# Two stacked graph layers on one core: V as three one-pass products, raw loaded behind P, graph 0 with rows first

## The chip, the cores and the metric

One Trainium2 chip, one core. The metric is the device time of one execution in microseconds (us), the median of several runs. A profile is one execution of its own.

## The reference, cut to what matters

Eight graphs (b) of C = 1024 nodes with D = 256 features, and an adjacency of 1024x1024 that is mostly zeros. All is float32.

```
L0:  H = (adj != 0); w = adj[0, :]                      # first row as edge weights
     Dn = 1 / (H @ w);  Be = 1 / H.sum(axis=0)
     conv(x, W, b) = Dn * (H @ (Be * (H.T @ (x @ W.T)))) + b
     h = layer_norm(relu(conv(x, W1, b1)), gamma, beta) # W1: 512x256
     y = conv(h, W2, b2) + x                            # W2: 256x512
x1 = layernorm(x + y)
L1:  agg = (adj @ x1) / max(adj.sum(-1), 1e-6)
     out = relu(concat(x1, agg) @ WL.T)                 # WL: 256x512
result = layernorm(x1 + out)
```

## The kernel before

Everything is tiled by 128 nodes: NT = 8 tiles a graph. The five engines each run an instruction order written out by hand, and wait for each other on semaphores; one engine's order is a queue that nothing overtakes. The stages of a graph, in TensorE's order, are these.

- **S1**: H transposed times x (x in two parts, x_hi and x_lo, each good for one pass of TensorE in the type float32r), one PSUM bank a tile. A column of ones beside x_hi gives the degrees for rBe. ScalarE copies a tile out as m_hi (`take_m_hi`), the vector engine as m_lo (`take_m_lo`).
- **S2**: HT (the transposed H) times m, in four jobs of 512 columns; split into z_high, z_low and z_cross.
- **M, P, TH, Q**, per tile: M is z_cross times W1_cross (two products), P is z_high times W1_high and z_low times W1_low (four products); `mm` writes 128x512 each. Together these six one-pass products give the exact float32 product. Then bias, relu, layer norm in the buffer hrow, its transposes (TH), and Q, the product with W2 in plain float32. The last three Q stand inside S3 (`last_of_Q`).
- **S3**: H times q (`take_q` on the vector engine, x_hi on ScalarE, x_lo on GpSimd), again out as m_hi and m_lo.
- **S4**: HT times m; the vector engine adds the residual (xres), makes bn_stats and bn_aggr, ScalarE the root (`root`), the vector engine its inverse and the centring (`centre`): this is x1, in xres. S4 computes tiles 0 and 1 together and then one tile after another. Ahead of the last tile's products TensorE transposes x1(0) and x1(1) (`before_last`).
- **V**: x1 transposed (TX, two transposes a tile) and copied to x1T by ScalarE, times WLT, in plain float32: two products a tile, each of which is two instructions in the trace. x1T has two slots. ScalarE copies the bank into yv.
- **L**: adjT times the right half of yv, in plain float32, and the final norm. The vector engine transposes the next graph's adjB blocks between.

Banks: PRODUCT_BANKS names the bank of each product. The transposes TH and TX take banks 6 and 7 in turn. A job waits until the bank's last user has been emptied (`free`, `emptied`, `full`). `over_graphs` loops over graphs; `more` is true for all but the last.

Beside this run the preparations for the next graph. SP issues the loads: w_row, x_in, then after the last Q raw (the 4 MB adjacency in the space that z and hrow leave, four pairs of tiles, four transfers each), then adjB tile by tile behind `H_ready` and `dn_ready`. The vector engine makes the degree sums (`sum_Dn`, a product of raw != 0 with w_row and a row sum): five among the last m_lo of S3, three during V. It also builds the eight H tiles (`build_H_tile`) during V. ScalarE splits the next x (`split_x_hi`) after S3, GpSimd subtracts (`split_x`) and later makes the residual.

Graph 0 has a setup of its own: it loads plain rows tile by tile, transposes them on TensorE (two sets of four 128x128 blocks a tile) between S1's products of tiles 0 to 5 (N_SIDE = 6 banks), and at places given by BETWEEN transposes the weights as well. Banks 6 and 7 are used in turn there too.

Of the kernel before, what the change touches and what calls it, by code (L numbers as in the profile page):

```python
# [11 lines left out]
P = 128  # L12
# [22 lines left out]
N_BANKS = 8  # L35
# [4 lines left out]
DN_LAG = 3  # L40


def graph_net(nc, x, adj, W1, b1, gamma, beta, W2, b2, WL, out):
# [21 lines left out]
    BETWEEN = {1: ("gamma",), 3: ("W1", "W1"), 5: ("WL", "WL"), NT - 1: ("W2", "W2")}  # L65
# [50 lines left out]
    for i in range(NT + 1):  # L116
        if i < NT:
            add_job("TX", i)
        if i > 0:
            add_job("V", i - 1)  # L120
    for i in range(NT):
        add_job("L", i)

    ctx = ExitStack()
    with ctx:
# [13 lines left out]
        H, _, _ = place("H", [P, NT, C], F32R)  # L139
# [3 lines left out]
        x_lo, _, _ = place("x_lo", [P, NT, D], F32R)  # L143
        m_hi, m_hi_at, _ = place("m_hi", [P, NT, D], F32R)
        m_lo, _, _ = place("m_lo", [P, NT, D], F32R)
        x_in, _, _ = place("x_in", [P, NT, D], F32)
        xres, xres_at, _ = place("xres", [P, NT, D], F32)
# [10 lines left out]
        x1T, _, _ = place("x1T", [P, 2, ND, P], F32, q_at)  # L158
        ident, _, _ = place("ident", [P, P], F32)
        small, _, _ = place("small", [P, 21, NT], F32)  # L160
# [13 lines left out]
        unread_V, _, _ = place("unread_V", [P, C], F32, nxt)  # L174
        unread, _, _ = place("unread", [P, C], BF16, q_at)

# [6 lines left out]
        W1T, _, _ = place("W1T", [P, ND, DH], F32, xres_at)  # L183

        def col(n):
# [3 lines left out]
         std_o, rstd_o, gb, rDn_main, rDn_cross, shift_h) = (col(n) for n in (*range(16), 18, 19, 20))  # L189
        gamma_c, bW2_c, eps_c = gb[:, 0:NH], gb[:, NH:NH + ND], small[:, 16, 0:1]  # L190
        stats, _, _ = place("stats", [P, NT, 6], F32)
# [3 lines left out]
        banks = [ctx.enter_context(nc.psum_tensor(f"bank{n}", [P, 512], F32)) for n in range(N_BANKS)]  # L195

        def sem(name):
# [10 lines left out]
        x_loaded, w_loaded, W2_loaded, W1_loaded, WL_loaded, gamma_loaded, beta_loaded, bias_loaded, table_loaded = (  # L208
            sem(n) for n in ("x_loaded", "w_loaded", "W2_loaded", "W1_loaded", "WL_loaded",
                              "gamma_loaded", "beta_loaded", "bias_loaded",  # L210
                              "table_loaded"))
        ident_zero, ident_ready, eps_ready, ones_ready, x_split, x_hi_done, xb_part, xb_ready = (
            sem(n) for n in ("ident_zero", "ident_ready", "eps_ready", "ones_ready", "x_split", "x_hi_done",
# [8 lines left out]
        W1_high_done, W1_low_done, W1_low_scaled, W1_cross_done = (  # L222
            sem(n) for n in ("W1_high_done", "W1_low_done", "W1_low_scaled", "W1_cross_done"))
# [61 lines left out]
        def _(sp):  # L285
            def load_graph(b):
                for j in range(NT // 2):
                    for a in range(NB):
# [35 lines left out]
            load_first_rows(4)  # L324
            load_first_x(3)
            load_first_rows(5)
            sp.dma_start(WLn[:, :, :], WL.rearrange("(t p) d -> p t d", p=P)).then_inc(WL_loaded, 16)
            load_first_rows(6)
            load_first_rows(7)
            sp.dma_start(W2n[:, :, :], W2.rearrange("(t p) d -> p t d", p=P)).then_inc(W2_loaded, 16)  # L330
            sp.dma_start(beta_row[:, :], beta.partition_broadcast(P)).then_inc(beta_loaded, 16)
            sp.dma_start(b1_row[:, :], b1.partition_broadcast(P)).then_inc(bias_loaded, 16)
            sp.dma_start(b2_row[:, :], b2.partition_broadcast(P)).then_inc(bias_loaded, 16)

            def graph(b, more, first):
                if more:
# [5 lines left out]
                    sp.wait_ge(*full("Q", NT - 1, b))  # L342
# [28 lines left out]
        def _(pool):  # L371
            nc.gpsimd.memset(ident[:, :], 0.0).then_inc(ident_zero, 1)
            nc.gpsimd.memset(x_hi[:, :, D:DP].bitcast(F32), 1.0).then_inc(ones_ready, 1)
            nc.gpsimd.memset(eps_c, NORM_EPS).then_inc(eps_ready, 1)
# [19 lines left out]
            for j in range(NT // 2):  # L394
                pool.wait_ge(first_x_loaded[j], 16)
# [33 lines left out]
        def _(act):  # L429
# [87 lines left out]
            def graph(b, more):  # L517
# [46 lines left out]
                if more:  # L564
                    split_x_hi(b + 1)
# [534 lines left out]
```

## Time and profile before

| | before |
|---|---|
| median of 3 runs | 1089.66 us (1089.65 to 1089.69) |
| profiled execution | 1090.12 us |
| its span, first to last instruction | 1088.5 us |
| mean granted TensorE clock | 0.999 of full speed |
| TensorE busy | 1073.5 us (99%) |
| vector engine, ScalarE, GpSimd busy | 746.4, 372.7, 217.5 us (69%, 34%, 20%) |
| chain that ended last, by engine | TensorE 91%, vector engine 6%, DMA 1% |

The profiled execution is about 1.6 us longer than its span (start and end of the program). In the profile PE is TensorE's products, PEld its weight loads, DVE the vector engine, ACT ScalarE, POOL GpSimd, SP the engine that issues most loads. A row's duration runs from the start of an instruction to its end; following instructions of the same engine overlap by some tenths of a microsecond, so the distance from one start to the next is what an instruction costs its queue. The same line can serve several stages, so rows are told apart by their tiles and shapes.

### The profile page before, as it was taken

Reading aid. Unit: us, or ns where it says so; the run is one execution under the profiler, and the core shown is the slowest. Engines: PE = TensorE matmul, PEld = TensorE weight load, DVE = VectorE, ACT = ScalarE, POOL = GpSimd, SP = SyncE. Lnnn points to the kernel's source line nnn. Section 1 sums busy time; section 2 is a strip of 40 time slices with the busy share of each in tenths; the row PEclk is TensorE's granted clock in tenths of the full one; section 3 lists DMA queues with packets and bytes.
Section 4 is the critical chain, followed back from the end, with each engine's and each line's share of the span. In section 5 each row is a group of like instructions: output and inputs, shape, how many; then the busy total and the mean of one; then the engine's idle time right before and its main releaser. Section 6 shows DMA issues by size and latency. Waiting matters only on the chain.

```text
span 1088.5 us, 18849 instructions
## 1 busy us (share of the span) xinstructions
PE 1073.5 (99%) x6235; PEld 919.3 (84%) x6235; DVE 746.4 (69%) x1972; ACT 372.7 (34%) x811; POOL 217.5 (20%) x276
## 2 busy tenths in 40 slices
PE   7899999999999999999999999999999999999997
PEld 7789698896988969898798978989789896888966
DVE  6875596665965768758687486774867747867326
ACT  5372213622145321453115431154302533026230
POOL 1623004220041202312032120411204120041000
PEclk9999999999999999999999999999999999999999
DMA  8207712076210662125611355115542065300001
GB/s 295 59 1 156 155 42 57 0 154 155 57 40 24 130 157 55 39 54 121 143 48 39 83 126 117 41 39 112 128 87 68 9 142 127 68 11 1 1 1 39
DMA packets 63871, 86.44 MB, mean 79 GB/s; under 512 B 8164, under 2 KB 53864, under 8 KB 63848
## 3 DMA queue, kind: packets, MB, share of 16 engines
q1 hardware_dynamic: 63376, 85.75, 34.4%
q10 hardware_dynamic: 472, 0.40, 0.1%
q8 instruction: 13, 0.21, 0.1%
q14 instruction: 10, 0.08, 0.0%
HBM read 77.73 MB, written 8.39 MB: 79 GB/s over the span
## 4 chain that ended last, share of the span: by engine, by line
PE 91%; DVE 6%; DMA 1%; issue 1%; ACT 0%; SPq 0%; DVEq 0%
PE bank L882 41%; PE bank L993 10%; PE bank L1056 10%; PE bank L975 10%; PE bank L912 8%; PE bank L1023 3%; PE bank L1028 3%; PE bank L1029 3%; PE bank L1001 3%; PE bank L1041 1%; DMA raw<-in_adj_dram 1%; DVE adjT L666 1%; DVE unread L618 1%; DVE HT L671 1%; DVE m_lo L653 1%
## 5 line engine op out<-in xcount | busy, mean ns | idle before, releaser
L882 PE MATMUL bank<-yv,adjT 128*128 128x257 f32 x1024 | 223.3, 379 | 0.0
L882 PEld LDWEIGHTS bank<-yv,adjT 128*128 128x128 f32 x1024 | 193.6, 189 | 31.8 <-issue 3.8
L469 ACT ACTIVATE small<-mv,small 128x1 f32<-128x1 f32 x192 | 56.6, 295 | 348.8 <-DVE mv L648 248.8
L403 POOL TENSOR_TENSOR xres<-x_in 128x256 f32<-128x256 f32 x64 | 45.6, 748 | 410.3 <-DMA out_dram<-xres 406.8
L882 PE MATMUL bank<-x_hi,H 128*128 128x256 f32 x512 | 126.0, 287 | 0.0
L912 PE MATMUL bank<-x_hi,H 128*128 128x258 f32 x512 | 123.8, 289 | 1.9 <-DVE x_lo L702 1.4
L882 PE MATMUL bank<-x_lo,H 128*128 128x256 f32 x512 | 122.4, 280 | 0.0
L993 PE MATMUL bank<-gW2T,xnT 128*128 128x256 f32 x512 | 122.1, 381 | 0.0
L882 PE MATMUL bank<-m_hi,HT 128*128 128x256 f32 x512 | 121.6, 280 | 0.0
L882 PE MATMUL bank<-m_lo,HT 128*128 128x256 f32 x512 | 120.9, 279 | 0.0
L912 PE MATMUL bank<-x_lo,H 128*128 128x256 f32 x512 | 119.3, 282 | 0.1
L1056 PE MATMUL bank<-WLT,x1T 128*128 128x512 f32 x256 | 119.1, 593 | 0.0
L464 ACT ACTIVATE m_hi<-bank,small 128x256 fp32r<-128x256 f32 x128 | 58.3, 477 | 164.1 <-DVE small L698 96.9
L993 PEld LDWEIGHTS bank<-gW2T,xnT 128*128 128x128 f32 x512 | 95.1, 189 | 13.4
L653 DVE SCALAR_TENSOR_TENSOR m_lo<-bank,small,m_hi 128x256 fp32r<-128x256 f32 x128 | 59.4, 480 | 68.4 <-ACT m_hi L464 68.4
L975 PE MATMUL bank<-HT,m_hi 128*128 128x512 f32 x256 | 101.2, 395 | 1.1 <-DVE m_lo L653 1.0
L975 PE MATMUL bank<-HT,m_lo 128*128 128x512 f32 x256 | 101.6, 397 | 0.0
L882 PEld LDWEIGHTS bank<-x_hi,H 128*128 128x128 f32 x512 | 96.8, 189 | 0.2
L882 PEld LDWEIGHTS bank<-x_lo,H 128*128 128x128 f32 x512 | 96.3, 188 | 0.2
L882 PEld LDWEIGHTS bank<-m_lo,HT 128*128 128x128 f32 x512 | 96.1, 188 | 0.0
L882 PEld LDWEIGHTS bank<-m_hi,HT 128*128 128x128 f32 x512 | 96.1, 188 | 0.0
L912 PEld LDWEIGHTS bank<-x_hi,H 128*128 128x128 f32 x512 | 93.4, 190 | 3.1 <-DVE H L603 2.3
(102 smaller groups left out, 1814.4 us busy)
## 6 DMA issues: line engine op xcount, KB each, us to landing
raw<-in_adj_dram SPq DMA_DIRECT2D x112, 256.0 KB, 8.6
adjB<-in_adj_dram SPq DMA_DIRECT2D x224, 128.0 KB, 3.4
x_in<-in_x_dram SPq DMA_DIRECT2D x31, 256.0 KB, 4.6
out_dram<-xres SPq DMA_DIRECT2D x108, 64.0 KB, 1.6
raw<-in_adj_dram SPq DMA_DIRECT2D x8, 512.0 KB, 10.4
w_row<-in_adj_dram SPq DMA_DIRECT2D x8, 512.0 KB, 3.7
out_dram<-xres SPq DMA_DIRECT2D x4, 256.0 KB, 2.2
W1n<-in_L_gnn_W_dram SPq DMA_DIRECT2D x1, 512.0 KB, 11.0
```

Source lines behind the costliest of these rows:

```text
L403: nc.gpsimd.tensor_tensor(xres[:, t, :], x_in[:, t, :], x_in[:, t, :], ALU.add).then_inc(xb_part, 1)
L464: nc.scalar.activation(m_hi[:, e, :], bank(stage, e)[:, 0:D], ACT.Identity, scale=rBe[:, e:e + 1])\
L469: nc.scalar.activation(std[:, i:i + 1], mv[:, which, i, 1:2], ACT.Sqrt, bias=eps_c)\
L653: empties_bank(nc.vector.scalar_tensor_tensor(out=m_lo[:, e, :], in0=bank(stage, e)[:, 0:D], scalar=rBe[:, e:e + 1], in1=m_hi[:, e, :].bit ...
L882: last = mm(bank(stage, i)[:, 0:n_cols], lhsT, rhs, start=(k == 0 and part == 0), stop=(k == NT - 1 and part == parts - 1))
L912: last = mm(*args, start=(c == 0 and n == 0), stop=(c == NT - 1 and n == 1))
L975: last = mm(bank("S2", job)[:, :], m[:, k, d * P:(d + 1) * P], HT[:, k, ch * CH:(ch + 1) * CH], start=(k == 0 and n == 0), stop=(k == NT - ...
L993: last = mm(bank("Q", i)[:, 0:D], xnT[:, k, :], gW2T[:, k, :], start=(k == 0), stop=(k == NH - 1))
L1001: last = nc.tensor.transpose(bank("TH", i)[:, k * P:(k + 1) * P], hrow[:, i % H_SLOTS, k * P:(k + 1) * P], ident[:, :])
L1023: last = mm(bank("M", s)[:, :], z_cross[:, d, nodes], W1_cross[:, d, :], start=(d == 0), stop=(d == ND - 1))
L1028: mm(bank("P", s)[:, :], z_high[:, d, nodes], W1_high[:, d, :], start=(d == 0), stop=False)
L1056: last = mm(bank("V", i)[:, :], x1T[:, i % 2, d, :], WLT[:, d, :], start=(d == 0), stop=(d == ND - 1))
```

## The change

V is split like M and P. WL becomes WL_high, WL_low and WL_cross once a graph (ScalarE and GpSimd, in the space of x_hi and x_lo, after S3), and x1 becomes x1_high, x1_low and x1_cross tile by tile in three slots: `take_x1` on ScalarE, `take_x1_low` on the vector engine (this one empties the TX bank), `take_x1_cross` on GpSimd. V takes four products, a new job VM two; yv is V's copy (times 1 + 1/4096) by ScalarE, less VM by the vector engine. x1(0) and x1(1) are transposed ahead of S4's last tile as before, x1(2) behind it, and then x1(i + 3) behind VM(i).

The centring of x1 (and of the result, except in the last graph) moves to ScalarE (`centre_rows`), with a shift from two small operations on GpSimd (`shift_of`). Six of the next graph's H tiles are built in S4 (H_LATE), two after V. raw's first three pairs are loaded behind the last P, the fourth behind the last Q. The degree sums: 0 ahead of q(7), 1 to 3 behind it, 4 to 7 around the last m_lo of S3 (DN_BEFORE). The split of the next x moves behind V.

In graph 0 the rows are loaded first and the weights last, and the weights' transposes stand in tiles 5 (W1), 6 (W2) and 7 (WL). W1_low and W1_cross are made by the vector engine, the residual by ScalarE (doubling) and GpSimd (b2). Degree sums 0 and 1 stand in the loop, 2 to 7 behind it, and six rBe are made in one go.

```diff
-    "V": (4, 5, 0, 1, 4, 5, 0, 1),
+    "V": (4, 0, 2, 4, 0, 2, 4, 0),
+    "VM": (5, 1, 3, 5, 1, 3, 5, 1),
...
+FIRST_DN = 2
+X1_SLOTS = 3
+H_LATE = 6
+DN_BEFORE = {4: (4,), 5: (5,), 7: (6,)}
...
-    BETWEEN = {1: ("gamma",), 3: ("W1", "W1"), 5: ("WL", "WL"), NT - 1: ("W2", "W2")}
+    BETWEEN = {1: ("gamma",), NT - 3: ("W1", "W1"), NT - 2: ("W2", "W2"), NT - 1: ("WL", "WL")}
...
+                    if j == 0:
+                        sp.wait_ge(*full("P", NT - 1, b - 1))
+                    elif j == NT // 2 - 1:
+                        sp.wait_ge(*full("Q", NT - 1, b - 1))
...
             load_first_rows(0)
+            load_first_rows(1)
             load_first_x(1)
-            load_first_rows(1)
             load_first_rows(2)
+            load_first_rows(3)
+            load_first_x(2)
+            load_first_rows(4)
             load_w(0)
-            load_first_x(2)
-            load_first_rows(3)
+            load_first_rows(5)
+            load_first_x(3)
+            load_first_rows(6)
             sp.dma_start(W1n[:, :, :], W1.rearrange("(t p) d -> p t d", p=P)).then_inc(W1_loaded, 16)
...
             load_first_rows(7)
...
+                for d in range(ND):
+                    pool.wait_ge(WL_high_done, b * ND + d + 1)
+                    nc.gpsimd.tensor_tensor(WL_low[:, d, :], WLT[:, d, :], WL_high[:, d, :].bitcast(F32),
+                                            ALU.subtract).then_inc(WL_low_done, 1)
...
+                def take_x1_cross(i):
+                    pool.wait_ge(*emptied("TX", i, b))
+                    n = i % X1_SLOTS
+                    nc.gpsimd.tensor_tensor(x1_cross[:, n, :], x1_high[n].bitcast(F32),
+                                            x1_low[:, n, :].bitcast(F32), ALU.subtract).then_inc(x1_cross_done, 1)
+
+                for i in range(NT):
+                    shift_of("1", 1, rstd_1, shift_1, mean_1_scaled, shift_1_done, i, b)
+                    if i >= NT - 2:
+                        take_x1_cross(i - (NT - 2))
+                for i in range(2, NT):
+                    take_x1_cross(i)
...
+                def take_x1(i):
+                    n = i % X1_SLOTS
+                    act.wait_ge(*full("TX", i, b))
+                    nc.scalar.activation(x1_high[n], bank("TX", i)[:, 0:D], ACT.Copy, scale=ROUND_DOWN)\
+                      .then_inc(x1_high_done, 1)
+                    nc.scalar.activation(x1_cross[:, n, :], bank("TX", i)[:, 0:D], ACT.Copy, scale=SPLIT * ROUND_DOWN)\
+                      .then_inc(x1_scaled, 1)
+
+                for i in range(NT):
+                    root("1", 1, std_1, i, b)
+                    if i > 0:
+                        centre_rows("1", rstd_1, shift_1, shift_1_done, i - 1)
+                    if i >= NT - 3:
+                        take_x1(i - (NT - 3))
+                centre_rows("1", rstd_1, shift_1, shift_1_done, NT - 1)
+                for i in range(NT):
+                    if i + 3 < NT:
+                        take_x1(i + 3)
+                    act.wait_ge(*full("V", i, b))
+                    empties_bank(nc.scalar.activation(yv[:, i, 0:2 * D], bank("V", i)[:, :], ACT.Copy,
+                                                      scale=1.0 + 1.0 / SPLIT), "V", i)
...
+                if c == NT - 3:
+                    sum_Dn(0, 0, unread, (first_rows_loaded[0], 16))
+                if c == NT - 2:
+                    sum_Dn(1, 0, unread, (first_rows_loaded[1], 16))
+                    take_W1_low(0)
+            take_W1_low(1)
+            sum_bW2()
+            take_W1_cross(0)
+            take_W1_cross(1)
+            sum_Dn(2, 0, unread, (first_rows_loaded[2], 16))
+            take_first_rBe()
+            take_m_lo("S1", 0, 0, 0)
             build_HT_columns(NT - 2)
...
+                next_Dn((0,), unread_Q)
                 take_q(NT - 1)
+                next_Dn((1, 2, 3), unread_Q)
...
                 for e in range(NT):
+                    if e in DN_BEFORE:
+                        next_Dn(DN_BEFORE[e], unread)
                     take_m_lo("S3", e, b, NT + e)
...
+                next_Dn((NT - 1,), unread)
+
+                def take_x1_low(i):
+                    n = i % X1_SLOTS
+                    dve.wait_ge(x1_scaled, b * NT + i + 1)
+                    empties_bank(nc.vector.scalar_tensor_tensor(
+                        out=x1_low[:, n, :], in0=bank("TX", i)[:, 0:D], scalar=SPLIT,
+                        in1=x1_cross[:, n, :].bitcast(F32), op0=ALU.mult, op1=ALU.subtract), "TX", i)
...
                         nc.vector.bn_stats(stats[:, i, :], xres[:, i, :]).then_inc(stats_done, 1)
-                    if i > 0:
-                        if i < NT:
+                    if i < NT:
+                        if more and 0 < i <= H_LATE:
                             dve.wait_ge(stats_done, b * NT + i + 1)
-                        centre("1", 1, xres[:, i - 1, :], rstd_1, i - 1, b)
-                    if i < NT:
-                        if i == 0:
+                            build_H_tile(i - 1, b + 1)
+                        elif i == NT - 1:
+                            dve.wait_ge(stats_done, b * NT + i + 1)
+                            take_x1_low(0)
+                        else:
                             dve.drain()
                         nc.vector.bn_aggr(mv[:, 1, i, :], stats[:, i, :]).then_inc(var_done["1"], 1)
-
+                take_x1_low(1)
+                take_x1_low(2)
                 nc.vector.memset(yv[:, :, 2 * D:YP], 1.0).then_inc(y_ones, 1)
...
+                transpose_x1(2)
+                pe.wait_ge(WL_cross_done, b * ND + ND)
 
                 for i in range(NT):
+                    n = i % X1_SLOTS
                     pe.wait_ge(*free("V", i, b))
                     pe.wait_ge(*emptied("TX", i, b))
                     for d in range(ND):
-                        last = mm(bank("V", i)[:, :], x1T[:, i % 2, d, :], WLT[:, d, :],
+                        part = slice(d * P, (d + 1) * P)
+                        mm(bank("V", i)[:, :], x1_high[n][:, part], WL_high[:, d, :], start=(d == 0), stop=False)
+                        last = mm(bank("V", i)[:, :], x1_low[:, n, part], WL_low[:, d, :],
+                                  start=False, stop=(d == ND - 1))
+                    fills_bank(last, "V", i)
+                    pe.wait_ge(*free("VM", i, b))
+                    pe.wait_ge(x1_cross_done, b * NT + i + 1)
...
+                    if i + X1_SLOTS < NT:
+                        transpose_x1(i + X1_SLOTS)
```

## Rows read from the trace of the kernel before

**Rows 1.** The page, busy time and share of the span by engine.
```profile
PE 1073.5 (99%) x6235; PEld 919.3 (84%) x6235; DVE 746.4 (69%) x1972; ACT 372.7 (34%) x811; POOL 217.5 (20%) x276
```

**Rows 2.** Windows, TensorE, S4 and V of graph 3: length, busy, clock, DMA.
```profile
494.70:510.15 15.45, 15.45 (x135) 1.00 0.49 105
510.15:525.20 15.05, 15.05 (x46) 1.00 0.70 164
```

**Rows 3.** Timeline, TensorE, into V of graph 3 (start, duration, what).
```profile
507.89 0.60 PE L1041 MATMUL bank<-ident,xres 128*128 128x128 f32 x4
510.15 1.88 PE L1056 MATMUL bank<-WLT,x1T 128*128 128x512 f32 x4
511.86 0.38 PE L1041 MATMUL bank<-ident,xres 128*128 128x128 f32 x2
```

**Rows 4.** Timeline, TensorE, two tiles of M and P of graph 3.
```profile
453.79 0.62 PE L1023 MATMUL bank<-W_cross,z_cross 128*128 128x512 f32 x2
...
455.18 0.60 PE L1001 MATMUL bank<-ident,hrow 128*128 128x128 f32 x4
...
469.72 0.71 PE L1023 MATMUL bank<-W_cross,z_cross 128*128 128x512 f32 x2
...
471.20 1.89 PE L993 MATMUL bank<-gW2T,xnT 128*128 128x256 f32 x8
```

**Rows 5.** Timeline, vector engine, S4 of graph 3.
```profile
503.02 0.45 DVE L801 SCALAR_TENSOR_TENSOR xres<-bank,small,xres 128x256 f32<-128x256 f32 x1
...
503.99 0.41 DVE L642 TENSOR_SCALAR xres<-xres,mv,small 128x256 f32<-128x256 f32 x1
...
504.41 0.45 DVE L801 SCALAR_TENSOR_TENSOR xres<-bank,small,xres 128x256 f32<-128x256 f32 x1
...
510.35 0.48 DVE L801 SCALAR_TENSOR_TENSOR xres<-bank,small,xres 128x256 f32<-128x256 f32 x1 [0.27 <-PE bank L882]
...
510.87 0.43 DVE L808 BATCH_NORM_STATS2 stats<-xres 128x6 f32<-128x256 f32 x1
511.33 0.41 DVE L642 TENSOR_SCALAR xres<-xres,mv,small 128x256 f32<-128x256 f32 x1
```

**Rows 6.** Groups by line and shape: busy us, mean ns | idle before.
```profile
L417 POOL TENSOR_TENSOR x_lo<-q_f,x_hi 128x256 fp32r<-128x256 f32 x64 | 43.4, 684 | 159.7 <-ACT x_hi L534 159.7
...
L579 ACT ACTIVATE yv<-bank 128x512 f32<-128x512 f32 x64 | 38.2, 597 | 59.7 <-PE bank L1056 59.7
...
L568 ACT ACTIVATE x1T<-bank 128x256 f32<-128x256 f32 x64 | 23.3, 376 | 0.3 <-PE bank L1041 0.3
```

**Rows 7.** Timeline, vector engine, setup, GpSimd at W_low (20.57 to 24.21).
```profile
23.02 1.75 DVE L603 TENSOR_SCALAR H<-raw 128x1024 fp32r<-128x1024 f32 x1
```

**Rows 8.** Timeline of the setup of graph 0: vector engine, then TensorE.
```profile
13.79 0.69 DVE L603 TENSOR_SCALAR H<-raw 128x1024 fp32r<-128x1024 f32 x1 [2.37 <-DMA raw<-in_adj_dram]
...
16.54 0.69 DVE L603 TENSOR_SCALAR H<-raw 128x1024 fp32r<-128x1024 f32 x1 [0.32 <-DMA raw<-in_adj_dram]
...
25.25 0.36 PE L912 MATMUL bank<-x_hi,H 128*128 128x258 f32 x1 [1.44 <-DVE x_lo L702]
...
33.37 0.44 PE L873 MATMUL bank<-ident,bW_wide 128*128 128x128 f32 x2 [1.43 <-DVE bW_wide L689]
...
37.10 0.40 PE L975 MATMUL bank<-HT,m_hi 128*128 128x512 f32 x1
...
49.78 0.74 PE L1023 MATMUL bank<-W_cross,z_cross 128*128 128x512 f32 x2
```

**Rows 9.** Timeline, SP's queue, then vector engine, loads of graph 4.
```profile
482.60 7.82 SPq L289 DMA_DIRECT2D raw<-in_adj_dram  x16
...
482.61 0.42 DVE L743 TENSOR_TENSOR q_f<-bank,bW_row 128x256 f32<-128x256 f32 x1 [2.76 <-PE bank L993]
...
487.13 1.66 DVE L653 SCALAR_TENSOR_TENSOR m_lo<-bank,small,m_hi 128x256 fp32r<-128x256 f32 x4 [4.10 <-ACT m_hi L464]
...
498.83 1.54 DVE L618 SCALAR_TENSOR_TENSOR unread<-raw,w_row 128x1024 bf16<-128x1024 f32 x1 [1.56 <-DMA raw<-in_adj_dram]
```

More of the change, by code:

```diff
@@ L173, in graph_net @@
         o_f32, _, nxt = place("o_f32", [P, 2, D], F32, nxt)
-        unread_V, _, _ = place("unread_V", [P, C], F32, nxt)
+        unread_Q, _, _ = place("unread_Q", [P, C], BF16, m_lo_at + 4 * D * (NT - 2))
         unread, _, _ = place("unread", [P, C], BF16, q_at)
+        WL_high, _, nxt = place("WL_high", [P, ND, 2 * D], F32R, x_lo_at)
+        WL_low, _, nxt = place("WL_low", [P, ND, 2 * D], F32R, nxt)
+        assert nxt <= x_lo_at + 4 * NT * D
+        WL_cross = [x_hi[:, 2 * d:2 * d + 2, 0:D] for d in range(ND)]
+        x1_high = [x_hi[:, 2 * ND + n, 0:D] for n in range(X1_SLOTS)]
+        x1_low, _, nxt = place("x1_low", [P, X1_SLOTS, D], F32R, H_at + 4 * C * H_LATE)
+        x1_cross, _, nxt = place("x1_cross", [P, X1_SLOTS, D], F32R, nxt)
+        assert nxt <= H_at + 4 * C * NT and 2 * ND + X1_SLOTS <= NT
         W1n, _, nxt = place("W1n", [P, NH, D], F32, m_hi_at)
@@ L193, in graph_net @@
         assert NT >= 2 * NH and at[0] <= nc.sbuf_usable_end, (at[0], nc.sbuf_usable_end)
-        banks = [ctx.enter_context(nc.psum_tensor(f"bank{n}", [P, 512], F32)) for n in range(N_BANKS)]
+        psum = ctx.enter_context(nc.psum_tensor("bank", [P, N_BANKS, 512], F32))
+        banks = [psum[:, n, :] for n in range(N_BANKS)]
         def sem(name):
@@ L564, in graph @@
+                centre_rows("1", rstd_1, shift_1, shift_1_done, NT - 1)
+                for i in range(NT):
+                    if i + 3 < NT:
[3 more added lines that the diff above has]
+                                                      scale=1.0 + 1.0 / SPLIT), "V", i)
                 if more:
+                    act.wait_ge(*full("VM", NT - 1, b))
@@ L565, in graph @@
                     split_x_hi(b + 1)
-                def take_x1T(i):
-                    act.wait_ge(*full("TX", i, b))
-                    empties_bank(nc.scalar.activation(x1T[:, i % 2, :, :].rearrange("p k c -> p (k c)"),
-                                                      bank("TX", i)[:, 0:D], ACT.Copy), "TX", i)
-                for i in range(NT - 2):
-                    root("1", 1, std_1, i, b)
-                take_x1T(0)
-                take_x1T(1)
-                root("1", 1, std_1, NT - 2, b)
@@ L576, in graph @@
-                root("1", 1, std_1, NT - 1, b)
-                for i in range(NT):
-                    act.wait_ge(*full("V", i, b))
-                    empties_bank(nc.scalar.activation(yv[:, i, 0:2 * D], bank("V", i)[:, :], ACT.Copy), "V", i)
-                    if i + 2 < NT:
-                        take_x1T(i + 2)
                 for i in range(NT):
@@ L587, in graph @@
                     root("o", 2, std_o, i, b)
+                    if more and i > 0:
+                        centre_rows("o", rstd_o, shift_o, shift_o_done, i - 1)
+                if more:
+                    centre_rows("o", rstd_o, shift_o, shift_o_done, NT - 1)
                 if not more:
@@ L788, in graph, with next_Dn @@
                         take_q(s - LAG_Q - 1)
+                def next_Dn(tiles, into):
+                    if more:
+                        for c in tiles:
+                            sum_Dn(c, b + 1, into, (raw_loaded[c // 2], (b + 1) * IN_B))
+                next_Dn((0,), unread_Q)
                 take_q(NT - 1)
+                next_Dn((1, 2, 3), unread_Q)
                 if more:
@@ L834, in graph @@
                         nc.vector.reciprocal(rdeg[:, i:i + 1], deg_safe[:, i:i + 1]).then_inc(rdeg_done, 1)
-                    if i > 0:
+                    if not more and i > 0:
                         centre("o", 2, xres[:, i - 1, :], rstd_o, i - 1, b)
```

170 lines of the change are left out of this document (99 added, 71 removed).

## The prediction, made before the changed kernel was run

> **What bounds the kernel now.** I read the page first: TensorE is busy 99% of the span [rows 1]. So only two things count: columns that TensorE streams, and places where it would have to wait for somebody. Then I read, by windows, the stage that the change rewrites and the one ahead of it, in graph 3. S4 takes 15.45 us and V 15.05 us, TensorE busy throughout at full granted clock [rows 2]. Then TensorE's timeline around V [rows 3]: the reader is to see that x1's first two transposes stand *before* the last tile of S4 (507.89), so that V starts at 510.15 with its operands already copied. Then the vector engine's timeline over the same stretch [rows 5], because the new V hangs on it, and last the setup of graph 0 [rows 8].
>
> **V's products.** Before, a tile of V takes 1.71 us (510.15 to 511.86) and two transposes 0.22 (eight tiles in 15.05, less six such pairs: 8 x 1.715) [rows 2, 3]. After, a tile is six one-pass products of 128x512. Exactly that mixture stands in the trace as M and P of one tile: 1.48 us where transposes go ahead (469.72 to 471.20), 1.39 us where none do (453.79 to 455.18) [rows 4]. Six of the new V's tiles follow transposes and two don't: 6 x 1.48 + 2 x 1.39 = 11.66, and with six pairs of transposes at 0.22 12.98 us. The products save 15.05 - 12.98 = **2.07 us a graph**, 16.6 in all.
>
> **The new wait ahead of V.** Now three tiles are transposed ahead, and TX's banks are two (6 and 7, in turn). The third, x1(2), goes into the bank of x1(0), and that bank is emptied by `x1_low(0)` on the vector engine. This instruction is written into the iteration of the *last* S4 tile, behind its addition and its bn_stats, and so behind the last matmul of S4. TensorE's queue is in order, so V(0) stands behind these transposes too. The price from before's rows [rows 5]: S4 is out at 510.15; the addition of tile 7 starts at 510.35; bn_stats at 510.87; what follows it starts at 511.33. Here `x1_low` takes that place, of the same form as the addition (PSUM and SBUF, 128x256), 0.48: done at 511.81, and TensorE goes on about 0.05 later. 511.86 - 510.15 = **1.7 us of waiting a graph** where there was none. Behind it wait all of V and L.
>
> **Is the vector engine in time for it?** It takes 1.39 us a tile of S4 (503.02 to 504.41), with the centring at 0.41 [rows 5]. The change sends the centring to ScalarE (shift by GpSimd) and puts an H tile of 0.69 (as at 13.79 [rows 8]) in its place for six tiles: 1.39 + 0.69 - 0.41 = 1.67 us, against the 1.93 that TensorE needs (15.45 us for eight tiles [rows 2]). It starts earlier too: before, the sum of a late raw tile kept it (it began at 498.83 and took 1.54 [rows 9]) although TensorE's first two tiles are out a quarter into S4, at about 498.5. Walked through from 498.5, tile 7 could start at 509.8, so there is 0.6 us in hand. But GpSimd now splits WL in this stretch, four operations of 128x512. An H tile that met such an operation in the setup took 1.75 us in place of 0.69 [rows 7, 8]. One H tile so hit puts tile 7 at 510.85, 0.5 late; none costs nothing. I take the middle, **0.25 us** in the seven graphs that build an H (the last has none). The Trainium skill, "GPSIMD Engine Reference", section "1. Specifications", has the two engines share their SBUF interfaces, with contention for vector instructions in a two-port mode or with two SBUF inputs; by that rule both the degree sums and the H tiles are exposed and the PSUM readers are not, so it would give the whole 0.5, 1.8 us more over the seven graphs than my middle.
>
> **Inside V.** Per tile ScalarE has two 128x256 copies and one 128x512 (0.38, 0.38, 0.60 at most), the vector engine 0.48 + 0.75, GpSimd one subtraction of 0.68 [rows 5, 6] (the subtraction of VM is not in the trace; I bound it by 0.48 for half the columns and twice that). All are under the period of 1.70. The loop that could bind: transposes full, `take_x1` 0.65, V's copy 0.50, the subtraction of VM 0.7, `x1_low` 0.48, hand-overs 0.2: 2.5 us, and TensorE asks for that bank two tiles later, after 3.1 to 3.4. GpSimd's shifts, two operations on one column a tile, are not in the trace: below the 0.68 of 256 columns, above nothing; even at 0.68 each they and the crosses fit into S4's tiles, and I take 0.2 each. So 0 here; if an edge is 0.5 longer than I think, the last tiles wait some tenths.
>
> **Steady sum:** 2.07 - 1.7 - 0.25 = 0.12 us a graph, seven times, and 0.37 for the last: 1.2 us gained.
>
> **Loads and degree sums.** raw's twelve loads of tiles 0 to 5 are issued behind P instead of behind the last Q. Before, SP issues from 482.60 and the fifth tile, of the third pair, is there at 498.83: 16.2 us for three pairs, 5.4 each [rows 9]. Started at P's end (471.2 [rows 4]), pairs land near 477, 482 and 487.5, the last near 493. Sum 0 goes into the 2.76 us of idle ahead of q(7), whose bank fills at 482.6: hidden. Sums 1 to 3 (1.2 to 1.3 us each) fill 483.0 to 487.0, where the engine was idle for 4.1 us until m_lo(0) at 487.13 [rows 9]. Sums 4 to 6 stand ahead of m_lo(4), (5), (7); the latter is done by 496, S4 wants it at 498.0. Cost nothing; uncovered (a load 3 us late) the S4 wait would be 1 us. SP's queue passes nothing else here. ScalarE's new centrings in L (0.5 each) delay stores, m_hi and the residual by about 0.5 us, with over 10 us of slack at z_cross, so nothing. The split of WL on ScalarE lies in its gap after m_hi.
>
> **Graph 0.** Before, S1 ends at 37.10 and M starts at 49.78 [rows 8]; in between S2 takes what it must plus a wait. TensorE's long waits in S1 after the first load are 1.44 for x_lo and 1.43 for bW2 [rows 8]. The loads: tile 3, 3.3 MB into the order, is there at 13.79, tile 4, 4.35 MB, at 16.54 [rows 8], so 0.37 MB a us. In the new order, by that rate, rows 5 land near 16.9, rows 6 near 19.0, W1 near 20.3, rows 7 near 21.7, W2 near 23. Rows are early, but TensorE, which needs some 2.3 us for a tile's twelve products and two sets of transposes, reaches W1's place in tile 5 at about 19.2 and waits a microsecond. The second W1 transposes need the bank that `W1_low(0)` empties, which the vector engine reaches behind H(6), x_lo, HT(4) and sum(1), at about 23.9: two microseconds more, and W2's wait 0.3. What the earlier rows give goes back: tiles 0 to 5 of S1 end at about 31.3, half a microsecond later than before. Then bW2 costs no wait any more, S1 ends near 35.4 (two tiles of 1.9 and bW2's 0.3), and S2 runs through until 46.7. M must wait for z_cross: from 31.3 the vector engine has rBe 0.4, the first m_lo behind its m_hi 0.9, two HT 1.2, seven m_lo 2.8, two rBe 0.6, five sums of 1.2 and rDn 0.95, so 44.1, and about 3 more for z_low and z_cross: 47.1. 49.78 - 47.1 = **2.7 us**, bounds 0 (the W1 wait doubled) and 4.5 (no new wait at all).
>
> **Sum.** 1.2 + 2.7 = 3.9 us. Against the profiled execution, 1090.12 us (span 1088.5 and 1.6 around it), that is 1086.2; the median of the runs lies 0.46 lower: **1085.8 us**, faster by 0.36%. 0.2% is 2.2 us, about what a measurement of this kernel tells from no change.
>
> **Rivals.**
> *The wait ahead of V is hidden.* Then the whole 16.6 and the 2.7 come in: 1070.4. For it: nothing but a misread order; against it the queue order and the bank turn. 0.04.
> *The vector engine is late in S4.* Place: the H tiles. If GpSimd's work stretches each of the last five by 0.25 (tile 1.92), tile 7 starts at 511.9, 1.55 late in place of 0.25: 7 x 1.3 = 9.1 more, 1094.9, slower. It decides from a lateness of 0.8 a graph on (then the 3.9 are gone), and is slower by over 0.2% from 1.1 on. For it: the 1.75 us H [rows 7], and 0.6 in hand only; against: four GpSimd operations of twice a 128x256 one (0.68 [rows 6]) begin near 496 and end before 503. 0.12.
> *Graph 0 gives nothing,* because W1 and W2 now stand at the busiest tiles: 1088.5, within 0.2%. For it: the W1_low order; against: bW2's wait vanishes. 0.2.
> *V starves inside,* 0.4 us a graph on its bank loop: 3.2 more, 1089.0, same. 0.06.
> The forecast, both terms about as worked out (1083 to 1087.4): 0.58.
>
> **Numbers.** Faster: 0.58 + 0.04 = 0.62; same: 0.2 + 0.06 = 0.26; slower: 0.12. The likeliest case's own range is 1083 to 1087.4; taking in graph 0 without gain, V starving and half of the late vector engine: 1080 to 1092.
>
> **What the next profile shows.** V's timeline: transposes of x1(2) with an idle of about 1.5 to 2.0 us, released by x1_low, once a graph; V from there 12.9 us with no further wait. If that idle is under 0.5, the first rival; if the vector engine's bn_stats of tile 7 starts over a microsecond after S4's last matmul, the second. S3 and S4 without waits for raw or m_lo. M of graph 0 at 47.1, and waits for W1n and W1_low in the setup. The prediction is wrong if V's six products take over 1.55 us a tile, or if the wait ahead of V is shared by a late x1_high.

## The result and the profile after

| | before | changed |
|---|---|---|
| median | 1089.66 us (1089.24 to 1089.81, 5 runs) | 1093.40 us (1093.15 to 1096.25, 5 runs) |
| profiled execution | 1090.12 us | 1093.15 us |
| its span | 1088.5 us | 1091.5 us |
| mean granted TensorE clock | 0.999 | 0.991 |

The ratio is 1.0043 [1.0032, 1.0054], here and below that of the mean times: slower by 0.43%, and by 0.34% if the medians are compared. 1085.8 was forecast, with a range up to 1092; the prediction was wrong, in sign and in range.

The page, where TensorE was 99% busy before [rows 1]:
```profile
PE 1060.7 (97%) x6363; PEld 950.1 (87%) x6363; DVE 788.0 (72%) x1974; ACT 466.2 (43%) x1027; POOL 341.4 (31%) x601
```
TensorE is busy for 12.8 us less, and yet the program takes 3.0 us longer. What TensorE waited for (line, releaser: total, times, longest):
```profile
PE bank L1160 <- DVE x_low L903: 14.7, 8, 2.0
PE bank L992 <- DMA raw<-in_adj_dram: 4.4, 1, 4.4
PE bank L992 <- DVE W_low L776: 2.7, 1, 2.7
PE bank L1142 <- DVE z_cross L844: 1.6, 1, 1.6
PE bank L1054 <- ACT adjT L524: 1.1, 1, 1.1
```
The first line is the wait ahead of V that the prediction named, once a graph. The other four belong to the setup of graph 0. The rest of the loss shows in windows of TensorE: S4 and then wait and V, of graph 2 (first two rows) and graph 3 (length, busy, clock, DMA), against 15.45 and 15.05 before [rows 2]:
```profile
365.34:380.80 15.46, 15.46 (x134) 1.00 0.42 102
380.80:396.96 16.16, 14.21 (x62) 0.89 0.48 98
498.75:514.21 15.46, 15.46 (x134) 1.00 0.40 103
514.21:528.91 14.70, 12.75 (x62) 1.00 0.52 106
```
S4 is what it was. In graph 3 wait and V take 14.70, which is 0.35 less than V alone before. In graph 2 the same work takes 16.16 at a mean granted clock of 0.89. The timeline of TensorE there, and the same place in graphs 3 and 5:
```profile
382.90 0.69 PE L1160 MATMUL bank<-ident,xres 128*128 128x128 f32 x2 [1.95 <-DVE x_low L903]
...
385.94 0.58 PE L1160 MATMUL bank<-ident,xres 128*128 128x128 f32 x2
...
516.32 0.44 PE L1160 MATMUL bank<-ident,xres 128*128 128x128 f32 x2 [1.95 <-DVE x_low L903]
...
518.07 0.38 PE L1160 MATMUL bank<-ident,xres 128*128 128x128 f32 x2
...
519.67 0.38 PE L1160 MATMUL bank<-ident,xres 128*128 128x128 f32 x2
...
781.35 0.44 PE L1160 MATMUL bank<-ident,xres 128*128 128x128 f32 x2 [1.49 <-DVE x_low L903]
```
The first tile of V is 1.75 us long in graph 3 (516.32 to 518.07) and 3.04 in graph 2 (382.90 to 385.94). For 3.4 us TensorE ran at 1.2 GHz instead of 2.4, a granted clock of 0.50. The clock fell behind the wait, in four graphs: of the eight V, the rows of graphs 0, 1, 2 and 4 show 0.87, the other four 1.00. The wait was 1.95 in the four, and also in graphs 3 and 6, which kept the clock; in graphs 5 and 7 it was 1.5. The low stretch of graph 2, then V of graphs 1 and 3:
```profile
382.90:386.30 3.40, 3.40 (x11) 0.50 1.13 228
...
249.30:262.20 12.90, 12.87 (x55) 0.87 0.38 83
516.30:529.00 12.70, 12.69 (x61) 1.00 0.42 86
```
The vector engine in S4 of graph 3, which before had 0.27 us to spare ahead of tile 7 [rows 5]:
```profile
502.49 0.48 DVE L911 SCALAR_TENSOR_TENSOR xres<-bank,small,xres 128x256 f32<-128x256 f32 x1 [1.40 <-PE bank L1001]
...
504.59 1.77 DVE L673 TENSOR_SCALAR H<-raw 128x1024 fp32r<-128x1024 f32 x1
...
514.87 0.45 DVE L911 SCALAR_TENSOR_TENSOR xres<-bank,small,xres 128x256 f32<-128x256 f32 x1
...
515.84 0.42 DVE L903 SCALAR_TENSOR_TENSOR x_low<-bank,x_cross 128x256 fp32r<-128x256 f32 x1
```
The first H tile meets GpSimd's split of WL and takes 1.77 us; the five behind it take 0.69 to 0.73. From there on the engine never rests, and tile 7's addition starts 0.66 us after the end of S4 (514.21), not 0.20.

**Where the time went**, in the profiled execution. From the start of M to the start of L, the four graphs with the low clock take 1.0 to 1.3 us more than before. Graphs 3 and 6 take 0.3 less, graphs 5 and 7 (where the wait is 1.49 and 1.50) 0.7 and 0.9 less: together 2.5 more. M of graph 0 starts 0.9 later. Between L of graph 0 and M of graph 1 the new kernel is 0.4 faster. That is 3.0, as measured.

### The profile page after: what moved, and what is told of

Its sections match the earlier page's. It is cut to its first block, busy times and chain, and to the rows that moved or that the text cites. A ratio compares the mean times of both kernels' runs of the same rounds, so it can differ in the third digit from the quotient of the medians.

```text
span 1091.5 us, 20067 instructions
## 1 busy us (share of the span) xinstructions
PE 1060.7 (97%) x6363; PEld 950.1 (87%) x6363; DVE 788.0 (72%) x1974; ACT 466.2 (43%) x1027; POOL 341.4 (31%) x601
## 4 chain that ended last, share of the span: by engine, by line
PE 88%; DVE 9%; issue 2%; DMA 1%; ACT 0%; SPq 0%; DVEq 0%; ACTq 0%
PE bank L1001 36%; PE bank L1031 10%; PE bank L1112 10%; PE bank L1094 10%; PE bank L1179 3%; PE bank L1186 3%; PE bank L1180 3%; PE bank L1142 3%; PE bank L1147 3%; PE bank L1148 3%; PE bank L1120 3%; DVE H L673 2%; DVE stats L918 2%; DVE xres L911 2%; PE bank L1160 1%
## 5 line engine op out<-in xcount | busy, mean ns | idle before, releaser
L436 POOL TENSOR_TENSOR x_lo<-q_f,x_hi 128x256 fp32r<-128x256 f32 x64 | 46.5, 732 | 159.8 <-ACT x_hi L578 159.8
L1001 PEld LDWEIGHTS bank<-x_lo,H 128*128 128x128 f32 x512 | 96.3, 188 | 0.2
L1031 PEld LDWEIGHTS bank<-x_lo,H 128*128 128x128 f32 x512 | 93.3, 190 | 0.2
```

The costliest lines, as they stand in the source:

```text
L436: nc.gpsimd.tensor_tensor(x_lo[:, i, :], q_f32[:, i % 2, :], x_hi[:, i, 0:D].bitcast(F32), ALU.subtract).then_inc(q_split, 1)
L1001: last = mm(bank(stage, i)[:, 0:n_cols], lhsT, rhs, start=(k == 0 and part == 0), stop=(k == NT - 1 and part == parts - 1))
L1031: last = mm(*args, start=(c == 0 and n == 0), stop=(c == NT - 1 and n == 1))
```

## The experiments

All are edits of the changed kernel. "Before" in a group was run on the same chip: 1089.8, 1089.9 and 1090.0 us in the three groups.

**e2_fill: keep TensorE busy in the wait.** Eight products whose result is overwritten are put into the wait; nothing that waits is changed.
```diff
+                pe.wait_ge(*free("V", 0, b))
+                for _ in range(8):
+                    mm(bank("V", 0)[:, :], HT[:, 0, 0:P], HT[:, 0, 0:CH], start=True, stop=True)
                 transpose_x1(2)
```


> The changed kernel with eight additional products of 128x512 between S4 and the transposes of x1(2), into the bank that V(0) overwrites; nothing reads them. The wait for x1_low stays, but TensorE works through 1.9 of its 2.2 us. Theory A: the clock stays at 1.00 in every V, the wait itself costs the same, so only the half clock is won back: 6.6 us of it in the profile of the changed kernel, hence 1086 to 1088 us. Rival (the half clock in V has another cause, for example the transposes or the denser one-pass products): the clock in V drops as before in about half the graphs, time 1093 or, if the products run into the wait's end, a little over.

Measured 1086.69 (1085.81 to 1087.01), ratio to before 0.9969 [0.9957, 0.9982]. Windows from the end of S4 over V, graphs 0 and 4 of it:
```profile
110.00:129.00 19.00, 18.89 (x106) 1.00 0.63 128
640.00:661.00 21.00, 20.89 (x105) 1.00 0.51 113
```
The granted clock is 1.00 in the very graphs in which it was 0.87, and in the other six V as well, while V of graph 0 starts where it did in the changed kernel (115.78 against 115.70). TensorE does more work and the program is 6.7 us shorter than the changed kernel by the medians, 8.0 by the means. The theory was right. That is the price of the low clock, and it alone turns a gain of 0.3% into a loss.

**e10_h5: one H tile less beside GpSimd.** H tiles start one iteration later in S4, so that none meets the split of WL; three are built after V.
```diff
-                        if more and 0 < i <= H_LATE:
+                        if more and 1 < i <= H_LATE:
...
-                            build_H_tile(i - 1, b + 1)
+                            build_H_tile(i - 2, b + 1)
```


> The changed kernel with the first H tile a tile later in S4 (tiles 0 to 4 at S4's tiles 2 to 6, three after V), so that no H tile meets GpSimd's split of WL. The wait ahead of V stays in kind. Theory (one H tile of 1.77 us in place of 0.69 makes the vector engine 0.5 us late at tile 7, the idle is 1.95 in place of 1.50, and only the longer one is followed by the half clock: graphs 5 and 7, at 1.49 and 1.50, kept theirs): idle 1.50 in all eight graphs, clock 1.00, 1093.4 - 6 x 0.45 - 6.6 = 1084 us. Rival (the half clock is not tied to that half microsecond): idle 1.50, clock down in about half of the graphs, 1090.5.

Measured 1083.21 (1082.99 to 1084.21), 0.9942 [0.9928, 0.9955]. The waits, and TensorE's timeline at V and at M of graph 0:
```profile
PE bank L1160 <- DVE x_low L903: 12.0, 8, 1.5
```
```profile
114.34 0.44 PE L1160 MATMUL bank<-ident,xres 128*128 128x128 f32 x2 [1.50 <-DVE x_low L903]
```
```profile
49.69 0.73 PE L1142 MATMUL bank<-W_cross,z_cross 128*128 128x512 f32 x2 [1.65 <-DVE z_cross L844]
```
The wait is 1.50 in all eight graphs and the granted clock 1.00 in all, as the theory had it (1084). One vector instruction of 0.69 us, moved away from its neighbour, goes with a gain of 10.2 us. Of these 2.7 are the wait (0.45 in six graphs) and about 6.5 the clock in V. The third part is no merit of the edit: M of graph 0 starts at 49.69 in place of 50.64 although the setup is the same. TensorE waits for W1_low(0) as long as in the changed kernel (2.69 and 2.70), but here the clock happened to stay at 1.00 behind it, and there it fell. The edit also takes one H tile out of S4. That the meeting counts and not the number of tiles is seen in graph 5 of the changed kernel, which builds six tiles, none of them slowed, and waits 1.49.

**e11_longer: a longer wait.** Two additions of 128x256 whose result nobody reads stand ahead of `x1_low(0)`.
```diff
+                            for n in range(2):
+                                nc.vector.tensor_tensor(o_f32[:, n, :], xres[:, i, :], b2_row[:, :], ALU.add)
                             take_x1_low(0)
```


> The changed kernel with two additions of 128x256 on the vector engine ahead of x1_low(0) (into o_f32, which nothing reads there): the wait ahead of V is made about 0.7 us longer and nothing else is changed. Theory (the half clock behind the wait comes with its length: kept at 1.5 us of idle, lost in about half of the graphs at 1.95): with 2.6 us of idle the clock drops in all or nearly all graphs, so 8 x 0.65 + 3 to 4 more drops of 1.65, 1103 to 1105 us. Rival (the drops are drawn at random whatever the length, about half of the graphs): 8 x 0.65 alone, 1098.5, clock as in the changed kernel.

Measured 1098.02 (1095.43 to 1098.35), 1.0069 [1.0055, 1.0083]. The waits, then windows of wait and V, graphs 0 and 1:
```profile
PE bank L1162 <- DVE x_low L903: 20.7, 8, 2.7
```
```profile
108.00:130.00 22.00, 19.34 (x108) 0.92 0.63 132
241.00:264.00 23.00, 20.34 (x124) 1.00 0.62 137
```
My theory, that a longer wait drops the clock more surely, fell: 2.65 us of idle dropped it in three graphs of seven (the eighth waited 2.17 and kept it), 1.95 in four of six. The rival, as many drops as before whatever the length, gave the time (1098.5). Its reason, a draw by lot, is not what the traces show; see the last section.

**e1_early: no wait ahead of V.** The first transposes of x1 go ahead of S4's tile 6 and their splits among tiles 4 to 7; four H tiles in S4, four after V.
```diff
-H_LATE = 6
+H_LATE = 4
...
-                    if i == NT - 1 and before_last:
+                    if i == NT - 2 and before_last:
...
-                        elif i == NT - 1:
+                        elif i in (NT - 3, NT - 2):
                             dve.wait_ge(stats_done, b * NT + i + 1)
-                            take_x1_low(0)
+                            take_x1_low(i - (NT - 3))
```


> The changed kernel with x1(0) and x1(1) transposed ahead of S4's tile 6 in place of tile 7, their x1_low on the vector engine in the iterations of tiles 5 and 6 (no longer behind tile 7's bn_stats), their crosses on GpSimd two tiles earlier, and four H tiles in S4 in place of six (four after V). Setup of graph 0 as changed. Theory A (the loss is the wait ahead of V, about 2.2 us a graph in TensorE's issue time, and the half clock behind it, 1.65 us in four of the eight graphs): both go, about 8 x 2.1 + 6.6 = 23 us, so 1070 us, no idle ahead of x1(2)'s transposes, clock 1.00 in every V. Rival B (V's new loop over three engines is the limit and the wait would only move inside V or to L): 1086 to 1093, with waits of TensorE for x1_low, x1_cross or the banks inside V. Rival C (H tiles built after V are now late for adjB and L): V as in A, but waits of the vector engine or TensorE at the end of L, over 1075.

Measured 1081.24 (1080.36 to 1081.58), 0.9921 [0.9908, 0.9935]. TensorE's timeline of graph 3, the vector engine's, and ScalarE's:
```profile
506.91 0.38 PE L1159 MATMUL bank<-ident,xres 128*128 128x128 f32 x2
...
513.22 0.44 PE L1159 MATMUL bank<-ident,xres 128*128 128x128 f32 x2 [1.06 <-DVE x_low L903]
```
```profile
512.14 0.69 DVE L936 TENSOR_TENSOR yv<-yv,bank 128x512 f32<-128x512 f32 x1 [0.71 <-ACT yv L639]
512.74 0.42 DVE L903 SCALAR_TENSOR_TENSOR x_low<-bank,x_cross 128x256 fp32r<-128x256 f32 x1
```
```profile
510.47 0.60 ACT L617 ACTIVATE xres<-xres,small 128x256 f32<-128x256 f32 x1 [0.28 <-POOL small L427]
...
511.51 0.60 ACT L639 ACTIVATE yv<-bank 128x512 f32<-128x512 f32 x1
```
Neither theory gave the time (1070, or 1086 to 1093): the wait ahead of V is gone, and a new one of 1.06 us stands inside V, ahead of x1(5). `x1_low(3)` stands in the vector engine's queue behind the subtraction of VM(0), and that waits for ScalarE's copy of V(0). The copy starts at 511.51, though TensorE was done with V(0) at about 508.2, because ScalarE still has S4's last root, its last two centrings and the copies of x1(3) ahead of it. The wait had moved.

**e7_swap: e1_early, and x1_low ahead of the subtraction.**
```diff
+                    if i + 3 < NT:
+                        take_x1_low(i + 3)
                     dve.wait_ge(*full("VM", i, b))
...
-                    if i + 3 < NT:
-                        take_x1_low(i + 3)
```


> The kernel of e1_early, and inside V the vector engine does x1_low(i + 3) ahead of the subtraction of VM(i) in place of behind it. Theory: e1_early's remaining wait, 1.06 us of idle a graph ahead of x1(5)'s transposes (7.9 us in all), is that of x1_low(3) behind VM(0), which waits for V(0)'s copy in ScalarE's queue; with the order changed it falls below 0.2 us a graph: 1081.2 - 7 = 1074 us, V 13.0 us from S4's end. Rival (ScalarE's queue itself is late: take_x1(3) is behind two centrings, and the wait only moves to the next tile or to the crosses): 1078 to 1081.

Measured 1072.82 (1071.79 to 1073.26), 0.9840 [0.9827, 0.9854], near the theory's 1074. What TensorE waits for, by the profile's list of waits:
```profile
PE bank L991 <- DMA raw<-in_adj_dram: 4.5, 1, 4.5
PE bank L991 <- DVE W_low L776: 2.7, 1, 2.7
PE bank L1141 <- DVE z_cross L844: 1.7, 1, 1.7
PE bank L1053 <- ACT adjT L524: 0.8, 1, 0.8
```
Only the setup is left. S4 and V of graph 3 take 28.39 us (488.67 to 517.06) in place of 30.50: 2.1 a graph, as much as was forecast for the products. That is partly luck. The products save 2.46 at full clock (below), and some 0.3 is lost in V in gaps too short for the list: two tiles there take 1.75 and 1.85 in place of 1.60 to 1.62.

**The setup: e3_w1, e4_oldsetup, then e8_swap_old, e9_swap_w1, e12_w1both.** e3 takes W1_low(0) ahead of HT(4) and sum(1) in graph 0; e4 puts graph 0's old setup into the changed kernel.
```diff
+                if c == NT - 2:
+                    take_W1_low(0)
                 if c >= 2:
                     build_HT_columns(c - 2)
```


> The changed kernel with W1_low(0) of graph 0 moved on the vector engine ahead of HT(4) and degree sum 1, 1.9 us earlier in its queue; nothing else. Theory A (TensorE's 2.7 us wait for the bank that W1_low(0) empties, at 24.73, is what sinks graph 0's setup, with the half clock behind it): the wait falls to 0.9 or less, the clock stays up, tiles 0 to 5 of S1 end 2.5 to 3.5 us earlier; M starts at 47.5 to 48.5 in place of 50.64, time lower by 2 to 3 us, 1090 to 1091.5. Rival (the vector engine's chain from its first rBe to rDn sets M's start whatever TensorE does): M's wait for z_cross grows by what S1 gains, M at 50.6, time 1093.

> The changed kernel with the whole setup of graph 0 as it was before (load order, places of the weights' transposes, W1 split by ScalarE and GpSimd, residual on GpSimd, degree sums and rBe in the old order); the eight graphs behind it as changed. If graph 0's new order lost 0.9 us (M at 50.64 against 49.78), this gives 1092.5; if it lost more further on (its residual or sums disturb graph 0 later), less, 1090 to 1091.5; if it was a gain that something else hid, over 1094. The half clocks ahead of V remain, so single runs vary by 3 us.

Measured e3 1093.82 (1092.2 to 1095.31), 1.0032 [1.0020, 1.0044]; e4 1094.52 (1092.6 to 1095.83), 1.0044 [1.0030, 1.0058]. M of graph 0 in e3, then in e4:
```profile
49.30 0.74 PE L1143 MATMUL bank<-W_cross,z_cross 128*128 128x512 f32 x2 [1.64 <-DVE z_cross L845]
```
```profile
49.20 0.74 PE L1151 MATMUL bank<-W_cross,z_cross 128*128 128x512 f32 x2
```
Both start M 1.3 to 1.4 us earlier than the changed kernel (50.64), and neither is faster: the clock fell in V in six graphs of e3 and in four of e4. By time these two are inconclusive, a microsecond drowns in drops of some 1.6 each. M itself is no firm measure either. With the setup unchanged it starts at 50.6 to 50.7 where the clock falls behind W1_low's wait (the changed kernel, e2, e7, e11), and at 49.69 and 49.95 where it doesn't (e10, e1); with the old setup it starts at 49.78, 49.80 and 49.20. So of e3's 1.3 us about 1.0 is the clock, which it kept: the wait of 2.70 has become one of 0.95 and, further on, one of 1.78. I asked again on e7, where the clock no longer falls in V: e8 is e7 with the old setup, e9 is e7 with e3's edit and sum(3) ahead of the rBe, e12 is e9 with W1_low(1) moved in too and sum(1) behind it.

> The kernel of e7_swap with the whole setup of graph 0 as it was before the change. There is no half clock in V any more, so the two setups can be told apart. Theory (the change's setup loses what the profiles say, M at 50.64 against 49.20 in e4_oldsetup): 1.4 us faster than e7_swap, or 1072.6 if that is at 1074. Rival (the new setup pays back later, in the residual or in the degree sums of graph 0): equal to e7_swap or slower.

> The kernel of e7_swap with W1_low(0) of graph 0 ahead of HT(4) and sum 1 (as in e3_w1), and degree sum 3 moved ahead of the first rBe, into the vector engine's idle there. Theory: W1_low(0) gives 1.3 us (M at 49.30 in e3_w1), and sum 3 takes 1.2 of the 1.6 us by which M waits for z_cross: M at 48.1, 2.5 us faster than e7_swap, so 1071.5 and 1 us faster than e8_swap_old. Rival (in e3_w1 the idle ahead of the first rBe has shrunk, so that sum 3 delays it): M at 49.3, 1.3 faster.

> The kernel of e9_swap_w1 with W1_low(1) of graph 0 ahead of HT(5) as well, and degree sum 1 behind it. Theory: the 1.78 us wait ahead of W2's first transposes (26.45 in e9_swap_w1) is W1_low(1) behind H(7) and HT(5) and the sum; it falls below 0.5, S1 ends 1.3 us earlier. But the vector engine had only 0.56 us of idle left ahead of the first rBe, so M comes only about 0.5 us earlier (47.6) and then waits 1 us for z_cross: 1070.2. Rival (the later sum 1 costs what W1_low(1) gives): M at 48.1, 1070.7.

| | median us | ratio to before | M of graph 0 |
|---|---|---|---|
| e7_swap | 1072.82 (1071.79 to 1073.26) | 0.9840 [0.9827, 0.9854] | 50.67 |
| e8_swap_old | 1072.82 (1072.26 to 1073.08) | 0.9841 [0.9828, 0.9855] | 49.80 |
| e9_swap_w1 | 1070.68 (1069.63 to 1070.81) | 0.9820 [0.9807, 0.9834] | 48.14 |
| e12_w1both | 1071.04 (1070.97 to 1071.12) | 0.9826 [0.9813, 0.9840] | 48.71 |

The new setup as changed is worth nothing: e7 equals e8 in time, and e8's theory (1.4 us faster) fell. The profile gives e8 0.9 at M and 0.5 in span, but 1.9 us of its executions lie outside the span, of e7's 1.6, and e7's profile is one in which the clock fell in the setup (0.50 from 26 to 28 us). With W1_low(0) first and sum(3) moved it is worth 2.1 (e9's theory had 2.5, with M at 48.1). M in e9, and the new wait of e12:
```profile
48.14 0.73 PE L1143 MATMUL bank<-W_cross,z_cross 128*128 128x512 f32 x2 [0.32 <-DVE z_cross L846]
```
```profile
34.67 0.39 PE L1032 MATMUL bank<-x_hi,H 128*128 128x258 f32 x1 [1.44 <-ACT bW_row L558]
```
In e9 z_cross is hardly late any more (0.32 for 1.65): against e3 (49.30, 1.64) that is sum(3). e12 brought nothing more, against a theory of M at 47.6: W1_low(1)'s wait fell from 1.78 to 0.36, and the next thing is late, the bias product bW2. e9_swap_w1 beats both kernels: 1.8% faster than before, 2.1% than the change.

## Why the prediction was wrong

**Products: right, and better.** Forecast 12.98 us for V from the transposes of x1(2) to L; at full clock 12.59 (516.32 to 528.91), and 1.60 for a tile with its transposes (518.07 to 519.67), forecast as 1.70. That is 2.46 saved a graph, for 2.07.

**The wait ahead of V: right in place, mechanism and nearly in size.** Forecast 1.7 for the order and 0.25 for lateness, 1.95; measured 2.11 from the end of S4 (514.21 to 516.32) in six graphs and 0.45 less in two. With the products this is a steady gain of 3.7 us at full clock (0.35 in six graphs, 0.8 in two), where 1.2 was forecast.

**The vector engine's lateness: the middle was mis-sized.** I had the two answers right, 0 or a tile hit, and took half. In the trace it is all or nothing: six graphs are hit, the tile takes 1.77 [rows 7 has 1.75], and tile 7 starts 16.12 us after the start of S4; the prediction's figure for a hit was 510.85 against 494.70, 16.15. The rule of the Trainium skill ("GPSIMD Engine Reference", section "1. Specifications") gave the whole 0.5 and was nearer than my middle: the addition is 0.66 - 0.20 = 0.46 late, and the trace agrees with 1.77 for an H tile beside GpSimd and 0.45 for the additions that read PSUM. The lateness of 1.1 from which the prediction called the kernel slower was not reached, so this rival, though it ends on the right side, is not what happened. Its own sum doesn't come out either: five tiles of 0.25 more each put tile 7 at 509.8 + 1.25 = 511.05, 0.7 late and not 1.55.

**The step that failed: "TensorE goes on about 0.05 later".** The sum priced the wait as its length alone. Behind it the clock fell in four graphs of eight, 1.5 to 1.7 us each in the profile and 6.7 us in the medians (e2). No term and no rival had it. With it the steady part is a loss of about 2.6 instead of a gain of 1.2. It was not to be ruled out from before's rows: TensorE was never idle in S4 and V there [rows 2], and the waits of 1.44 and 1.43 in the setup [rows 8], behind which the granted clock was 1.00, say nothing of one of 1.95. Against the forecast for the profiled execution (1086.2, measured 1093.15) the miss of 7.0 us is made up of about 6.3 for the clock in V and 3.6 for graph 0, less 2.5 by which the steady gain was better than forecast and 0.4 behind graph 0's L.

**Graph 0: also failed.** Forecast M at 47.1, measured 50.64, before 49.78. The setup on TensorE:
```profile
24.73 1.08 PE L992 MATMUL bank<-ident,W1n 128*128 128x128 f32 x4 [2.70 <-DVE W_low L776]
...
26.04 1.06 PE L992 MATMUL bank<-ident,raw 128*128 128x128 f32 x4
...
37.63 0.40 PE L1094 MATMUL bank<-HT,m_hi 128*128 128x512 f32 x1
...
50.64 0.73 PE L1142 MATMUL bank<-W_cross,z_cross 128*128 128x512 f32 x2 [1.65 <-DVE z_cross L844]
```
The wait for W1_low(0) was foreseen at two microseconds and is 2.70; behind it the clock is low here too (four transposes 1.08 for 0.60 at 20.27), until about 27.7, some 1.5 us. So S2 starts at 37.63, not at 35.4, and then z_cross is 1.65 late, not 0.4. The step that failed here has two parts: the clock behind the wait, again left out (e10, which kept it, starts S2 at 36.69 and M at 49.69), and the vector engine's chain up to z_cross, which was put too short. The rival "graph 0 gives nothing" named the W1_low order. That is part of the reason: with W1_low(0) first M starts at 49.30 (e3), and with sum(3) out of the chain as well at 48.14 (e9). The last 1.0 us to the forecast 47.1 stays unexplained.

**Loads and degree sums: right at nothing.** TensorE waits for no raw tile and no m_lo in S3 and S4. Sums 1 to 3 stand between q(7) and m_lo(0):
```profile
486.67 0.42 DVE L837 TENSOR_TENSOR q_f<-bank,bW_row 128x256 f32<-128x256 f32 x1 [1.62 <-PE bank L1112]
...
491.19 1.66 DVE L719 SCALAR_TENSOR_TENSOR m_lo<-bank,small,m_hi 128x256 fp32r<-128x256 f32 x4
```
**Inside V: right only because V came late.** The changed kernel has no wait there. With V on time a wait of 1.06 us a graph appears (e1), more than the prediction's edge ("the last tiles wait some tenths") and at x1(5). The loop of 2.5 us holds V's copy and the subtraction of VM at their own lengths. What it left out is where ScalarE stands when V starts: the last root and two centrings of 0.6 are still ahead of V(0)'s copy in its queue.

## What to carry to other kernels

A new wait on an engine that never waited is worth more than its length: price what its clock does behind it, at both levels, and give that case a chance of its own. When a part is to be judged whose worth is near a microsecond, first remove the losses that come and go from the kernel that carries it (e7), look for those that are left (its setup), and only then change the part. And where an instruction either meets a neighbour or doesn't, take one of the two ends and move it out of the way (e10), not their mean.

## What the runs showed of the hardware

**The clock behind a wait.** Behind 1.50 us of idle ahead of V the clock stayed at 2.4 GHz each of 12 times (the changed kernel, e3, e4, e10). Behind 1.95 it fell to 1.2 GHz in 14 of 20. Behind 2.65 in 3 of 7. Each fall in V meant 3.0 to 3.4 us of V at the low level, and 1.3 to 1.7 us of time. The start of V in graph 0 of the changed kernel:
```profile
115.70:116.60 0.90, 0.90 (x5) 1.00 1.13 221
116.70:120.00 3.30, 3.30 (x11) 0.50 1.13 225
```
The length of the wait doesn't decide alone. In the setup, the same wait for W1_low(0) of 2.7 us was followed by the low clock in four traces (the changed kernel, e2, e7, e11) and by the full clock in e10. In e4 the clock fell in the setup behind waits of 1.21 and 0.56; in e8, with the same setup and the same two waits, it held:
```profile
32.71 0.44 PE L1001 MATMUL bank<-ident,bW_wide 128*128 128x128 f32 x2 [1.21 <-DVE bW_wide L773]
...
34.41:38.00 3.59, 3.58 (x17) 0.52 0.00 0
```
Nor is it a draw by lot. From the end of the wait to the fall it is 0.99, 0.48 and 0.03 us in graphs 0, 1 and 2 of the changed kernel; graph 3 is spared, and graph 4 has 0.91 (read off windows of 0.1 us). In e3 it is 1.21, 0.81 and 0.38, then a spared graph, then 1.16, 0.74 and 0.35; in e4, from graph 2 on, 0.96, 0.51 and 0.07, a spared graph and 0.90. So the fall comes earlier from graph to graph until one is spared. That speaks for the place of the wait in time as the second condition beside its length, and against the three counts above as chances of a length. It is not shown: no run here was made that shifts V in time alone. The Trainium skill, "TensorE: Matmul & The Clock Gate", section "What's actually happening", describes a gate that follows how busy TensorE has been and whose count doesn't start with the kernel; that would fit falls that wander like this, and no run here tests it.

**Who pays when two engines meet.** In graph 3 the H tile beside GpSimd's 128x512 operations took 1.77 us. In graph 5 an H tile began inside the same GpSimd operations, and this time they gave way. Vector engine, then GpSimd:
```profile
770.09 0.69 DVE L673 TENSOR_SCALAR H<-raw 128x1024 fp32r<-128x1024 f32 x1
```
```profile
503.46 2.35 POOL L445 TENSOR_TENSOR x_hi<-x_hi,WL_low 128x512 fp32r<-128x512 f32 x2
...
768.95 2.88 POOL L445 TENSOR_TENSOR x_hi<-x_hi,WL_low 128x512 fp32r<-128x512 f32 x2
```
GpSimd's pair took 2.88, for 2.35 in graph 3, and the H tile its usual 0.69. That graph's wait was 1.49, and its clock held. In both graphs the H tile starts 1.13 to 1.14 us after the pair, near the joint of its two operations, and in graph 3 it takes 1.08 longer, nearly one of them (half of 2.35). Which of the two gets going first would explain both outcomes; the traces don't show it.
